# A two-layer attention and feed-forward kernel on one core: another order of the work at the four stage borders

## What is computed

```python
def _L0_xattn_ref(hidden_states, encoder_hidden_states, attention_mask, Wq, bq, Wk, bk, Wv, bv, Wo, bo):
    q = (hidden_states @ Wq.T + bq)      # 16 heads of 16
    k = (encoder_hidden_states @ Wk.T + bk); v = (encoder_hidden_states @ Wv.T + bv)
    scores = jnp.einsum('bhnd,bhtd->bhnt', q, k) * scale + attention_mask[:, None, :, :]
    out = jnp.einsum('bhnt,bhtd->bhnd', jax.nn.softmax(scores, axis=-1), v)
    return out @ Wo.T + bo
def _L0_ffn_ref(x, proj_w, anchors, routing_temp, w1, w2):
    expert_weights, q = _router(x, proj_w, anchors, routing_temp)   # tanh, distance to anchors, top 2 of 6, softmax
    h = jax.nn.gelu(jnp.einsum('btd,edh->bteh', x, w1))
    return jnp.einsum('bteh,ehd,bte->btd', h, w2, expert_weights)
def _L1_xattn_ref(q, kv, mem, w_q, w_kv, w_concat):                 # one key and value head for 16 query heads
def _L1_ffn_ref(x, w1, b1, w2, b2):                                 # 256 -> 1024 -> 256, quantized piecewise gelu
x = x + _L0_xattn_ref(_layernorm(x, axis=-1), ctx_1024, mask_BxSxS2_ff0, ...)
x = x + _L0_ffn_ref(_layernorm(x, axis=-1), ...)
x = x + _L1_xattn_ref(_layernorm(x, axis=-1), ctx_1024, ctx_1024, ...)
x = x + _L1_ffn_ref(_layernorm(x, axis=-1), ...)
```

## Time and profile before

| | us |
|---|---|
| median of 3 runs (890.9 to 894.1) | 892.53 |
| the profiled execution's own time | 892.31 |
| its span | 890.5 |
| PE busy in the span | 783.8 |
| DVE busy | 660.3 |
| ACT busy | 520.1 |
| POOL busy | 397.4 |

### The profile page before, as it was taken

How to read it: one execution, slowest core, us unless ns; L and a number is a source line. 1 busy time by engine, 2 the same in 40 slices (tenths; PEclk the granted TensorE clock), 3 DMA queues, 4 the chain that set the end, 5 groups by cost and what they waited for, 6 DMA issues and landing times.

```text
span 890.5 us, 13722 instructions
## 1 busy us (share of the span) xinstructions
PE 783.8 (88%) x4452; PEld 577.4 (65%) x4452; DVE 660.3 (74%) x1576; ACT 520.1 (58%) x942; POOL 397.4 (45%) x323
## 2 busy tenths in 40 slices
PE   4789999999886999999978988888878989999996
PEld 2556566666555787877854455444457878888885
DVE  6468777777756777877776888888757788977774
ACT  4245655555452446554435666566658777788774
POOL 3623322213213344344310222222138999899995
PEclk9989999999998999999968999999989999999999
DMA  8855533455200000001055555654000000000001
GB/s 291 124 108 107 136 63 74 86 105 99 68 0 1 1 1 6 2 1 49 1 73 73 73 72 73 120 72 68 8 1 1 1 24 25 25 24 1 24 24 49
DMA packets 24817, 48.01 MB, mean 54 GB/s; under 512 B 3655, under 2 KB 6856, under 8 KB 24234
## 3 DMA queue, kind: packets, MB, share of 16 engines
q1 hardware_dynamic: 22792, 42.87, 26.1%
q10 hardware_dynamic: 1954, 4.26, 1.3%
HBM read 11.47 MB, written 4.19 MB: 18 GB/s over the span
## 4 chain that ended last, share of the span: by engine, by line
PE 53%; DVE 17%; POOL 8%; issue 7%; ACT 6%; DMA 6%; ACTq 1%; SPq 0%; DVEq 0%; POOLq 0%
PE bank L135 16%; PE bank L371 5%; PE bank L396 5%; PE bank L777 5%; PE bank L629 5%; PE bank L421 5%; PE bank L407 4%; DMA qst<-mt 4%; POOL eex L508 3%; DVE mx L327 3%; PE bank L399 2%; POOL fy L696 2%; DVE x L597 2%; PE bank L121 2%; DMA qst<-ml 2%
## 5 line engine op out<-in xcount | busy, mean ns | idle before, releaser
L301 ACT ACTIVATE pt<-bank 77x512 f32<-77x512 f32 x256 | 146.3, 589 | 125.8 <-PE bank L399 76.9
L327 DVE TENSOR_REDUCE mx<-bank 128x4 f32<-128x308 f32 x256 | 110.0, 472 | 38.3 <-PE bank L374 24.9
L396 PE MATMUL bank<-qst,l_kst 128*77 128x512 f32 (+1 forms) x256 | 106.6, 431 | 20.8 <-DMA qst<-mt 13.3
L696 POOL TENSOR_TENSOR fy<-fpart,fg 128x512 f32<-128x512 f32 x64 | 103.1, 1611 | 9.3 <-DVE fpart L737 4.7
L371 PE MATMUL bank<-l_kblk,qh 128*128 128x308 f32 x256 | 91.5, 372 | 14.7 <-DVE mx L327 13.5
L103 POOL TENSOR_TENSOR rstd<-var,minus_half 128x4 f32<-128x4 f32 x32 | 32.7, 1023 | 139.4 <-DVE var L98 90.2
L689 POOL TENSOR_TENSOR frise<-fg,fg 128x512 f32<-128x512 f32 x64 | 90.6, 1415 | 9.0 <-POOL fy L696 4.6
L396 PEld LDWEIGHTS bank<-qst,l_kst 128*77 128x77 f32 (+1 forms) x256 | 36.8, 149 | 85.0 <-issue 49.8
L371 PEld LDWEIGHTS bank<-l_kblk,qh 128*128 128x128 f32 x256 | 50.6, 198 | 58.0 <-issue 50.8
L277 POOL TENSOR_TENSOR ol<-ot,oh 128x512 fp32r<-128x512 f32 x32 | 43.1, 1345 | 97.8 <-ACT oh L306 63.3
L597 DVE SCALAR_TENSOR_TENSOR x<-bank,eweight,x 128x256 f32<-128x256 f32 x192 | 79.6, 476 | 5.4 <-PE bank L629 5.1
(11 more groups left out here) (179 smaller groups left out, 2162.0 us busy)
## 6 DMA issues: line engine op xcount, KB each, us to landing
qst<-qh SPq DMA_DIRECT2D x64, 256.0 KB, 6.4
qst<-ql SPq DMA_DIRECT2D x32, 256.0 KB, 9.3
out<-x SPq DMA_DIRECT2D x8, 512.0 KB, 2.6
qst<-ml SPq DMA_DIRECT2D x8, 480.0 KB
x<-in_x ACTq DMA_DIRECT2D x3, 1024.0 KB, 11.0
weights<-in_mlp_w SPq DMA_DIRECT2D x2, 1024.0 KB, 5.1
mraw<-in_mask SPq DMA_DIRECT2D x8, 154.0 KB
x<-in_x SPq DMA_DIRECT2D x2, 512.0 KB, 5.8
```

Source lines behind the costliest of these rows:

```text
L301: self.nc.scalar.activation(self.pt[0:T, i // 4 % 2, i % 4, :], self.bank_of(G, i)[0:T, :], ACT.Exp).then_inc(self.probs, 1)
L327: self.nc.vector.reduce_max(out, banks[u % len(banks)][:, 0:4 * T].rearrange("q (p par t) -> q p par t", p=2, par=2), AX.X).then_inc(self. ...
L396: last = self.nc.tensor.matmul(out, layer.kst[rows, layer.stack(c * HC + 2 * k + par), b * T:(b + 1) * T], self.qst[rows, self.slot(G), c ...
L696: self.nc.gpsimd.tensor_tensor(self.y[:, k % 2, :], self.part[:, k % 2, :], self.g0[:, k % self.R, :], ALU.add).then_inc(self.y_ready, 1)
```

## The change

No instruction's work changes; the order of the lists does, with the semaphores that this needs. By engine:

- SP: tiles 8 to 15 of `x` (1,024 KB) are loaded right behind tiles 4 to 7, the other 2,048 KB behind the second mask load; before, ACT's queue issued all three. The copies for block 0 are queued as: mask's low parts, key half 0, query half 0, key half 1, maxima, query half 1. Before: all keys, both query halves, mask's low parts, maxima.
- PE at the start: block 0's `max_unit`s and `turn_maxima` come right behind its queries; the value projection (12 matmuls) and the transposes of block 1 come behind them. The wait for the keys is split in halves, the second in front of head 8.
- DVE at the start: the rest of `kh` (`kl`) moves behind `norm.rest`, and `moments` of block 1 behind block 0's 16 reductions.
- ACT at the start: `norm`, `lead` and `leading` of block 0 come ahead of the two copies into `kst` (L1081 of before). Its wait for `kblk_more` and `kst_in` moves to block 1, head 3.
- POOL at the start: the memset of `pt` comes ahead of `invert` of block 1.
- First attention to experts: `project`, `squash`, `compare` and `router` of expert block 0 come earlier by some pieces on PE, ACT and DVE.
- Experts to second attention: the 16 `max_unit`s of block 8 run on four banks instead of two, and without `output` and `add` of expert 5 in their middle; the two `add`s follow the reductions.
- Second attention to feed-forward: `early` of steps 0 and 1 moves ahead of the last two divisions.

The diff, cut to what moves:

```diff
-        FIRST_MAX1 = (ps[6], ps[7])
+        FIRST_MAX1 = (ps[6], ps[7], ps[2], ps[3])
...
                 sp.dma_start(x[:, NT:2 * NT, :], d["x"][:, NT:2 * NT, :]).then_inc(x1_in, 16)
+                sp.dma_start(x[:, 2 * NT:4 * NT, :], d["x"][:, 2 * NT:4 * NT, :]).then_inc(x2_in, 16)
+
+                att.stack_low(sp, 0)
                 sp.wait_ge(kst_clear, 1)
                 sp.wait_ge(kt_ready, 1)
...
-                                         part[64 * par:64 * par + 64, c, :].bitcast(F32)).then_inc(kst_in, 16)
-                for c in range(C):
-                    att.stack_queries(sp, 0, c)
-                att.stack_low(sp, 0)
+                                         part[64 * par:64 * par + 64, c, :].bitcast(F32)).then_inc(kst_in[c], 16)
+                    if c == 0:
+                        att.stack_queries(sp, 0, 0)
+                att.stack_maxima(sp, 0)
+                att.stack_queries(sp, 0, 1)
                 att.load_mask(sp, 1, d["mask"])
-                att.stack_maxima(sp, 0)
+                for b in range(2, B):
+                    tiles = slice(2 * b * NT, 2 * (b + 1) * NT)
+                    sp.dma_start(x[:, tiles, :], d["x"][:, tiles, :]).then_inc(xr_in, 16)
...
                 att.mask_parts(pool, 0)
-                norm.invert(pool, 1)
                 nc.gpsimd.memset(att.pt[64:P, :, :, :], 0.0).then_inc(pt_clear, 1)
                 pool.wait_ge(pt_clear, 1)
+                norm.invert(pool, 1)
...
                 nc.scalar.activation(l0.wqh[:], wq0, ACT.Copy).then_inc(wqh_ready, 1)
+                norm.norm(act, 0)
                 act.wait_ge(c_in, 32)
+                nc.scalar.activation(att.id5[:], id5f[:], ACT.Copy).then_inc(id5_ready, 1)
+                for c in range(C):
+                    norm.lead(act, 0, c, att.W[c], att.xh)
+                for c in range(C):
+                    att.leading(act, 0, c)
...
+                att.maxima(act, 0, FIRST_MAX[0])
+                norm.norm(act, 1)
                 act.wait_ge(v_clear, 2)
...
-                norm.norm(act, 1)
+                for c in range(C):
+                    norm.lead(act, 1, c, att.W[c], att.xh)
                 act.wait_ge(vo_in, 64)
...
                         if h == 3 and p >= 0:
+                            if p == 0:
+                                act.wait_ge(kblk_more, H)
+                                for c in range(C):
+                                    act.wait_ge(kst_in[c], 16 * 6)
                             att.lead_quotient(act, p, 0)
...
                 ex.gelu(act, 0, 0)
+                ex.squash(act, 0)
                 att.lead_quotient(act, BLOCKS - 1, 1)
                 ex.gelu(act, 0, 1)
-                ex.squash(act, 0)
...
-                nc.vector.tensor_tensor(l0.kl[:], l0.kt[:], l0.kh[:].bitcast(F32), ALU.subtract).then_inc(kt_ready, 1)
                 for c in range(C):
                     norm.rest(dve, 0, c, att.W[c], att.xh, att.xl)
+                nc.vector.tensor_tensor(l0.kl[:], l0.kt[:], l0.kh[:].bitcast(F32), ALU.subtract).then_inc(kt_ready, 1)
...
+                att.take_maxima(dve, 0, range(16), FIRST_MAX)
                 dve.wait_ge(x1_in, 16)
                 norm.moments(dve, 1)
-                att.take_maxima(dve, 0, range(16), FIRST_MAX)
...
-                for e in range(2):
-                    ex.rest(dve, 0, e)
+                ex.rest(dve, 0, 0)
+                ex.router(dve, 0)
+                ex.rest(dve, 0, 1)
...
-                for c in range(C):
-                    att.rest(dve, BLOCKS, c)
-                ex.add(dve, BLOCKS - 1, 4)
-                att.take_maxima(dve, BLOCKS, range(0, 8), FIRST_MAX1)
-                ex.add(dve, BLOCKS - 1, 5)
-                att.take_maxima(dve, BLOCKS, range(8, 16), FIRST_MAX1)
+                att.rest(dve, BLOCKS, 0)
+                att.take_maxima(dve, BLOCKS, range(0, 4), FIRST_MAX1)
+                att.rest(dve, BLOCKS, 1)
+                att.take_maxima(dve, BLOCKS, range(4, 16), FIRST_MAX1)
+                for e in (4, 5):
+                    ex.add(dve, BLOCKS - 1, e)
...
+                    if n == 2 * BLOCKS:
+                        ff.early(dve, 0)
                     att.divide(dve, G, 2)
+                    if n == 2 * BLOCKS:
+                        ff.early(dve, 1)
...
-                ff.early(dve, 0)
-                ff.early(dve, 1)
...
                 att.weigh(pe, l0, BLOCKS - 1, 3)
-                ex.hidden(pe, 0, 2)
                 pe.wait_ge(ex.router_ready, 1)
                 pe.wait_ge(att.unfolded, 4 * BLOCKS)
                 ex.project(pe, 0)
+                ex.hidden(pe, 0, 2)
+                pe.wait_ge(att.probs, H * BLOCKS)
+                ex.compare(pe, 0)
                 ex.hidden(pe, 0, 3)
...
-                for u in range(8):
-                    att.max_unit(pe, l1, BLOCKS, u, FIRST_MAX1)
-                ex.output(pe, BLOCKS - 1, 5)
-                for u in range(8, 16):
+                pe.wait_ge(ex.hh_ready, E * BLOCKS)
+                for u in range(16):
                     att.max_unit(pe, l1, BLOCKS, u, FIRST_MAX1)
                 att.turn_maxima(pe, BLOCKS, FIRST_MAX1[0])
+                ex.output(pe, BLOCKS - 1, 5)
```

More of the change, by code:

```diff
@@ L1435, in _ @@
                     norm.turn(pe, 1, c, att.W[c])
[L1436 to L1442 removed]
+                pe.wait_ge(kst_in[0], 16 * 6)
                 pe.wait_ge(kst_const, 2)
```

41 lines of the change are left out of this document (14 added, 27 removed).

## The result

The changed kernel took **866.49 us** (median of 4 executions, 865.0 to 867.44) where the kernel before took 893.32 beside it (890.9 to 894.1). The ratio is 0.9714, with an interval of 0.9694 to 0.9734. Forecast were 872.0, with 865 to 880. The sign and the range held. In the profiled execution (866.98) the span went from 890.5 to 865.2, by 25.3.

What follows compares the result with a forecast made beforehand. One engine is full in each stage's middle, so waits at the four borders were taken as what can be gained: -5.8 - 7.0 - 4.0 - 3.2 = -20.0 against 892.3 gives 872.3 us; range 865 to 880.

Steps and rivals of the forecast that it cites:

- Start, -5.8: Border ahead of block 0: 5.8 us saved, bounds -4.0 and -8.4; POOL's mh binds, PE idles 3 to 4 at head 3.
- The steps to the first maxima: Start: transposes at 12.65, queries at 16.1, second ql ends at 22.9, DVE's reductions end at 29.9 instead of 42.14.
- Start, transfers: Start: the maxima's copy, queued at about 31, lands near 35 to 36, hidden by PE's value products; cost taken: nothing.
- if the maxima's copy lands after 38: Start: a sign listed as showing the forecast wrong; the copy was expected near 35 to 36.
- First experts, -7.0: First attention to experts: router path starts earlier, compare at 258.7, 7.0 us saved; bounds -4.9 and -9.1.
- the clock holds: Rival at start and experts: PE idles less and keeps its clock; experts -9.1, total about 867; chance 0.13.
- The port lock: Rival at first experts: POOL's power holds DVE's ehl until its end; term -4.9, total about 874.5; chance 0.05.
- Block 8, -4.0: Experts to second attention: four banks, reductions at 0.435 each end at 455.7; 4.0 us saved, bounds -3.0 and -5.1.
- -5.1 (score alone): Block 8: the bound with the largest gain, 5.1 us, counting the score alone.
- Feed-forward, -3.2: Second attention to feed-forward: ACT no longer idles for early, DVE's fpart moves 3.2 us earlier; bounds -2.0 and -3.5.
- The middles: Insides of the stages: one engine is full, work unchanged, taken as 0; clock falls may land differently, 1.3 us each.
- start gives little: Rival at start: POOL's key products stretch or block 1's mask lands late; -0.8, total 877; chance 0.17 with experts' clock fallen.

Runs made afterwards that it cites:

- t_hold: Changed kernel with SP issuing the second query half, block 1's mask and last x tiles only once the maxima's copy has landed: 865.91 us (0.9698).
- t_keys: Changed kernel with six key transfers (the second key half) queued behind the maxima's copy instead of ahead of it: 865.7 us (0.9694).
- p_mask: Changed kernel with POOL's three mask instructions of block 1 moved ahead of the wol subtraction: 865.84 us (0.9706).
- v_half: t_keys plus the load of block 1's mask ahead of the maxima's copy and that mask's parts between POOL's key products: 869.0 us (0.9741).
- v_early: v_half with POOL's 16 key products beside DVE's reductions, ahead of invert of block 1: 869.16 us (0.9739).

## Why the prediction was right, and where not

**Start, -5.8: the size right (-6.2), the mechanism wrong.** The steps to the first maxima held within 1.2 us: queries at 16.1 (15.90), reductions done at 29.9 (28.72), because 16 took 6.24 and not 6.96. The 6.96 had been misread as the reductions' own pace: before, the first ones stepped at 0.51 us, behind matmuls at half clock, and those from the seventh on at 0.39. The step that failed is "Start, transfers": "the maxima's copy, queued at about 31, lands near 35 to 36" and "Cost taken: nothing". It landed at 40.57. I had counted only what stands ahead of it, at a mean rate. With nothing behind it (t_hold) it landed at 35.65, inside the forecast's 35 to 36, although it was queued 1.4 us sooner than forecast. So what the step left out is mainly what is queued behind the copy, 4.5 us here, and for 1 to 2 us more the tail of one or two engines. "if the maxima's copy lands after 38" stood in the list of what would make the forecast wrong, and it did. That the term's size came out is luck: POOL's limit, correctly placed at 46 to 47, lay only 2 us ahead of the place to which the late copy brought PE: t_keys shows exactly the forecast idling at head 3 (3.4 us) and the fall to 0.50 behind it. The change has such a fall too, only ahead of block 0.

**First experts, -7.0: the mechanism right, the term mis-sized (-9.7).** The rival "the clock holds" came true here, beyond its bound of -9.1. PE idled 0.89 and 1.49 us where it had idled 1.94 and 6.74, and the clock stayed at 1.00, to which the 2.1 that the path leaves open are put down. Power took 4.48 and not 4.70, though DVE worked beside it, and the rest of the 0.5 us left over isn't assigned. I had taken the clock as lost because it had been lost before, at a place where the change itself removed the idling.

**The port lock: against it.** The second `ehl` of DVE (259.24, 0.69 us) ran inside the power (255.56 to 260.04) as in the earlier trace rows, and the power kept its 4.48. DVE's small key products are held up by POOL's work, below.

**Block 8, -4.0: mis-sized (-5.2).** The reductions were taken at 0.435 each, which is the misread mean of block 0 again. They took 0.39 with four banks, which is 0.7 of the 1.2. (The mask matmul that block 0 has beside each is not the reason: with it they took 0.39 as well, 6.24 for 16, in the changed kernel.) The rest is covered by PE's transposes at full clock, 1.04 in place of the 1.91 of the earlier trace rows. One sign of the forecast did not come: block 9's queries were to follow expert 5's `output` without a wait for the maxima, but PE idled 1.55 us for them, so the bound "-5.1 (score alone)" is what came.

**Feed-forward, -3.2: right** (-3.1, and -2.6 to -3.0 alone). ACT loads its table right behind the quotient.

**The middles.** The sum took them as neutral and kept 1.3 for each fall that might land elsewhere. Two falls of before went and one came, which gave 1.6 in all, and 0.4 came back in the feed-forward. Without the 2.1 of the experts' clock and this 1.6 the sum would have met the result within 2 us.

**The rival "start gives little"** had the right cause in sight, transfers behind the copies, but placed it at block 1's mask. It was one copy of 32 KB. The mask was close all the same: in the change its load landed at 44.31, 0.8 us before POOL came to it, and in p_mask and t_hold POOL waited for it. v_half shows that the case lay close: with block 1's copies queued 7 us sooner it came about.

## What to carry to other kernels

When a border is shortened, look for the next two limits and ask how far apart they are. Here the maxima's copy, POOL and the load of the next mask stood within 2 to 3 us, and the copy's or POOL's delay removed alone gave nothing; with both removed, and the mask loaded sooner, another limit came up that cost more. Price a copy by everything that is in flight with it, behind it as well, and keep the large loads that nobody awaits behind the small ones that an engine awaits. Where a change removes an idle stretch, ask whether a fall of the clock goes with it: at the experts that was 2.1 of 9.6 us.

## What was not expected of the hardware

- A 32 KB copy queued at 30.03 into full DMA engines landed 10.5 us later; with nothing queued behind it, 6.1 us (t_hold); with little ahead of it and much behind, 3.3 (t_keys).
- A share of one to three of 16 DMA engines worked on for 2 to 4 us after the others had run dry (0.07 to 0.18), and the last copy landed at the end of it (t_hold, v_half).
- DVE's 16 small key products (one input on the chip) took 2.79 us alone, 4.86 beside POOL's memset, and 6.27 beside that and POOL's products, which themselves took 10.37 beside them and 10.58 without. They are not slowed evenly but held: in the changed kernel two of them stood until 18.95 and 19.00, when POOL's memset ended at 18.90, and in v_early those begun behind a product of POOL ended just behind it (20.40 behind 20.35, 21.06 behind 21.00). This is the row of before:

```profile
19.04 2.79 DVE L1245 TENSOR_SCALAR l_kblk<-l_kh,hsel 128x77 fp32r<-128x77 f32 x16
```

The Trainium skill, SBUF — State Buffer, section "Who interferes with whom", names this instruction of VectorE among those that can take the port pair shared with GpSimd. The trace agrees with it, and with an exclusive lock, by the ends just given. The same page counts reductions among those that don't contend. The trace agrees: beside POOL's products all but three of the steps were 0.39 us, as without them, and the three long ones, which make the 0.38 between 6.24 and 6.62, were behind PE's matmuls at half clock.
